# A Perceiver layer on one core: constant products in TensorE's fold, another order at its end, and row clearing moved into tile 0

## The reference

```python
# cross attention, 16 heads of 128
q_hk = (ln(x) @ Wq.T).reshape(b, s, H, K)
q_r = (q_hk @ w_kc_q) @ W_qr                   # 192, then 64 wide
kv_rope = kv_c * cos + rotate_half(kv_c) * sin # 257 rows of 64 for each batch
attn = softmax(q_r @ (kv_rope @ W_kr).T)
x = x + ((attn @ kv_rope) @ w_kc_kv.T).reshape(b, s, H * K) @ Wo.T
# self attention, weights are codes * scales (blocks of 32 rows)
x = x + softmax(q @ k.T / sqrt(128)) @ v @ wo + bo
# 64 experts, top 8, capacity 128: rows are scattered to their experts,
# put through gate, up and down, weighted and summed
x = x + moe(ln(x))
```

## Time and profile before

| | |
|---|---|
| median of 3 runs | 736.1 us (734.83 to 737.74) |
| profiled execution | 734.79 us |
| its span, first to last instruction | 733.0 us |
| PE busy | 631.6 us, 86% |
| DVE, ACT, POOL busy | 61%, 39%, 38% |
| mean granted clock of PE | 0.925 |
| chain that ended last | PE 52%, DVE 17%, issue 11%, ACT 8% |

### The profile page before, as it was taken

The page is one execution under the profiler, slowest core; times in us unless marked ns, Lnnn a source line. Parts: engine busy times, 40 slices in busy tenths (PEclk is TensorE's granted clock), DMA queues, the critical chain, the costliest instruction groups (busy, mean ns, idle before and its releaser), DMA issues.

```text
span 733.0 us, 16840 instructions
## 1 busy us (share of the span) xinstructions
PE 631.6 (86%) x6395; PEld 540.9 (74%) x6395; DVE 446.3 (61%) x1257; ACT 285.6 (39%) x788; POOL 275.1 (38%) x296
## 2 busy tenths in 40 slices
PE   5998687989989999999999999998886899999900
PEld 3887556977887896896897896896765688778800
DVE  1143696555677577677677677576573245555548
ACT  1112485336337337337347337346030043333300
POOL 3852599211212612612612612403103435555520
PEclk9556798999999999999999999999999999999965
DMA  7697551990400600500500200100002769998467
GB/s 192 191 250 185 164 190 35 293 325 4 138 2 2 199 2 9 193 2 10 192 3 10 77 3 10 56 3 31 32 4 86 203 196 334 330 318 277 131 254 296
DMA packets 90383, 95.85 MB, mean 131 GB/s; under 512 B 26047, under 2 KB 82104, under 8 KB 89280
## 3 DMA queue, kind: packets, MB, share of 16 engines
q1 hardware_dynamic: 83552, 78.40, 35.8%
q0 software_dynamic: 6144, 15.96, 6.0%
q10 hardware_dynamic: 608, 0.42, 0.2%
HBM read 60.19 MB, written 36.18 MB: 131 GB/s over the span
## 4 chain that ended last, share of the span: by engine, by line
PE 52%; DVE 17%; issue 11%; ACT 8%; DMA 4%; SPq 4%; POOL 2%; another core or an unknown queue 1%; POOLq 0%; DVEq 0%; ACTq 0%
PE bank L1258 6%; PE bank L1259 6%; PE bank L1260 6%; PE bank L1324 4%; PE bank L1292 3%; PE bank L1373 3%; PE bank L1278 3%; PE bank L1543 3%; PE bank L1313 3%; DMA Wh<-expert_rows 2%; POOL pair_rows L650 2%; ACT diag L735 2%; PE bank L1511 2%; ACT qspace L676 2%; DVE space L1212 2%
## 5 line engine op out<-in xcount | busy, mean ns | idle before, releaser
L697 ACT ACTIVATE pr<-bank,nmax 128x257 f32<-128x257 f32 x128 | 61.4, 480 | 95.5 <-DVE nmax L921 92.5
L574 POOL DMA_INDIRECT expert_rows<-h,slot x64 | 63.0, 984 | 69.4 <-DVE slot L1018 53.7
L1258 PE MATMUL bank<-space,Wh 128*128 128x128 f16 x512 | 88.1, 219 | 0.3
L1260 PE MATMUL bank<-space,Wl 128*128 128x128 f16 x512 | 88.1, 219 | 0.0
L1259 PE MATMUL bank<-space,Wh 128*128 128x128 f16 x512 | 88.1, 219 | 0.0
L557 POOL TENSOR_TENSOR Cr<-C,Ct 128x192 f32<-128x192 f32 x64 | 39.3, 636 | 122.4 <-PE bank L1324 113.3
L650 POOL DMA_INDIRECT pair_rows<-Wh,etok x64 | 62.4, 974 | 56.5 <-issue 36.2
L921 DVE TENSOR_REDUCE nmax<-bank 128x1 f32<-128x257 f32 x128 | 53.4, 421 | 43.0 <-PE bank L1306 30.1
L705 ACT COPY pT<-bank 128x256 f32<-128x256 f32 x128 | 47.6, 372 | 64.1 <-PE bank L1313 61.5
L1324 PE MATMUL bank<-Cr,pT 128*128 128x64 f32 x512 | 72.2, 264 | 0.1
L1324 PEld LDWEIGHTS bank<-Cr,pT 128*128 128x128 f32 x512 | 68.2, 194 | 0.2 <-ACT pT L705 0.2
(11 more groups left out here) (208 smaller groups left out, 1548.2 us busy)
## 6 DMA issues: line engine op xcount, KB each, us to landing
expert_rows<-h SPq DMA_DIRECT2D x8, 1120.0 KB, 13.3
Wh<-expert_rows SPq DMA_DIRECT2D x64, 140.0 KB
pair_rows<-zrow SPq DMA_DIRECT2D x8, 1024.0 KB
Wl<-L_ffn_gate_up_proj_dram SPq DMA_DIRECT2D x36, 192.0 KB
ring<-L_ffn_gate_up_proj_dram SPq DMA_DIRECT2D x28, 192.0 KB
space<-pair_rows SPq DMA_DIRECT2D x5, 1024.0 KB, 9.2
Wl<-L_ffn_down_proj_dram SPq DMA_DIRECT2D x36, 96.0 KB
C<-ctx_dram SPq DMA_DIRECT2D x24, 128.0 KB
```

What stands on the lines that cost most here:

```text
L574: e.indirect_dma_start(XE[:, :], bass.IndirectOffsetOnAxis(ap=slot[:, k:k + 1], axis=0), h3[:, :], None, bounds_check=E * CAP - 1, oob_is_ ...
L697: e.activation(pr[:, s, :], bank[r % 2][:, 0:NL], ACT.Exp, bias=nmax[:, s:s + 1], accum_out=rsum[:, s:s + 1]).then_inc(expd, 1)
L1258: e.matmul(dst, ah, bh, start=first and n == 0, stop=False)
L1260: ins = e.matmul(dst, al, bh, start=False, stop=last and n == len(terms) - 1)
```

## The change

It has six parts. PE: `keep_busy(n, to)` issues n products of two constant tiles (128 x 128, bfloat16) into `bank[1]`, which nobody reads; 4 between every two heads of the Q and M stages in all four groups (24 for each group), and 14, 14, 20 and 12 in rows 17 to 20 of tile 0. PE: `qb` moves from ahead of tile 0 to its row 2, behind the scores of rows 0 and 1. Parts: group 2 has part 0 alone, the last group parts 1 to 4, of which part 4's multiply and high half move into row 1 of tile 0 (DVE and ACT), ahead of `qb`'s low half on DVE; the multiplies of parts 1 and 2 now surround `kt0`'s low half. POOL: `rope_products(1)` moves from tile 0 to between the low halves of parts 0 and 1. SP: `load_context(1)` moves ahead of part 1's load, and the eight `blank` ahead of the wait for 16 parts and of the experts, each with a wait on `expd`. DVE: the split of `bv` moves into the last group.

```diff
+KEEP_AT = {17: 14, 18: 14, 19: 20, 20: 12}
-FOLD_PARTS = (0, 0, 2, 3)
+FOLD_PARTS = (0, 0, 1, 4)
# SP
             load_fold_first(3)
+            e.wait_ge(roped, 2 * BT)
+            load_context(1)
             load_part(1)
...
-            e.wait_ge(roped, 2 * BT)
-            load_context(1)
-
             e.wait_ge(f_m, GROUPS)
...
             load_codes(PARTS - 1, late[10], late_in[10])
 
-            e.wait_ge(w_done, PARTS)
-
...
+            e.wait_ge(iotas, 2)
+            for n in range(E // 8):
+                e.wait_ge(expd, 6 + 2 * n)
+                blank(n)
+
+            e.wait_ge(w_done, PARTS)
             for n in range(NB):
                 load_expert(n, n)
             for i in range(2, T):
 
                 e.wait_ge(roped, i * (2 * BT))
                 load_context(i)
-                if i == 2:
-                    e.wait_ge(iotas, 2)
-                    for n in range(E // 8):
-                        blank(n)
# POOL
-            for u in range(PART0[GROUPS]):
+            part_low(0)
+            rope_products(1)
+            for u in range(1, PART0[GROUPS]):
                 part_low(u)
...
-                if not last:
+                if not last and i != 0:
                     rope_products(i + 1)
# ACT
+                        if isinstance(i, int) and i == 0 and r == 1:
+                            x_use(XNEXT[-1], 0)
+                            part_high(LATE - 1)
...
-                for u in range(PART0[g], PART0[g + 1]):
+                for u in range(PART0[g], min(PART0[g + 1], LATE - 1)):
                     part_high(u)
-
-            x_use(XNEXT[-1], 0)
# DVE
+                        if isinstance(i, int) and i == 0 and r == 1:
+                            part_mul(LATE - 1)
+                            x_low(XNEXT[-1], 0)
...
                 if g == GROUPS - 1:
-                    for name in XNEXT[1:-1]:
-                        x_low(name, 0)
-                if len(left) > 2:
                     part_mul(left.pop(0))
+                    x_low("kt0", 0)
+                    part_mul(left.pop(0))
+                    x_low("qa", 0)
# PE
+            def keep_busy(n, to):
+
+                for _ in range(n):
+                    e.matmul(to[:, 0:P], ones16[:, :], before[:, :], start=True, stop=True)
...
+                        if isinstance(i, int) and i == 0 and r == 2:
+
+                            e.wait_ge(f_md, GROUPS)
+                            e.wait_ge(f_na, GROUPS)
+                            x_use("qb", 0)
...
+                        if isinstance(i, int) and i == 0 and r in KEEP_AT:
+                            keep_busy(KEEP_AT[r], bank[1])
...
# Q stage, and the same behind each head of the M stage
+                    if h < GH - 1:
+                        keep_busy(4, bank[1])
```

More of the change, by code:

```diff
@@ L1146, in _ @@
                     part_mul(left.pop(0))
+                if g == GROUPS - 1:
+                    e.wait_ge(rwT_ready, 3)
+                    e.tensor_copy(bvh[:, :], bvT[:, :]).then_inc(bv_split, 1)
+                    e.wait_ge(bv_split, 1)
+                    e.tensor_tensor(bvl[:, :], bvT[:, :], bvh[:, :], ALU.subtract).then_inc(bv_split, 1)
                 e.wait_ge(f_m, g + 1)
@@ L1152, in _ @@
                     next_h1(0)
-                for u in left:
-                    part_mul(u)
-            x_low(XNEXT[-1], 0)
+                if g < GROUPS - 1:
+                    for u in left:
+                        part_mul(u)
             e.sem_inc(h3_free, FREE)
             e.wait_ge(iotas, 2)
[L1160 to L1163, removed]
             tile(0, None, None)
@@ L1514, in _ @@
                     transposes(g + 1)
-            e.wait_ge(f_md, GROUPS)
-            e.wait_ge(f_na, GROUPS)
-            x_use("qb", 0)
             tile(0, None, None)
```

## The result

| | before | after |
|---|---|---|
| median | 735.47 us (734.19 to 737.74) | 751.9 us (749.25 to 756.88) |
| ratio of after to before | | 1.0202, 95% interval 1.0158 to 1.0246 |
| profiled execution | 734.79 us | 749.25 us |
| its span | 733.0 us | 747.5 us |
| mean granted clock | 0.925 | 0.930 |

The change makes the kernel 2% slower; the forecast was 745, range 735.5 to 752. The profiled executions differ by 14.46 us, and all but 0.6 of that is there at tile 1's out product.

The account below looks back on a forecast made before the run. The prediction took TensorE (PE), busy 86% of 733.0 us, as the bound, with POOL setting tile 0's length. Its terms, 0 + 2 + 0 - 2 + 12 + 2 - 5 = +9 us on 734.8, gave 743.8, written as 745; range 735.5 to 752.

Parts of the forecast that it names:

- (e): Head of tile 1: context load held behind clearings 6 and 7 delays POOL and PE; +12 us, ends 10 and 14.
- (f): Tile 1: PE idles some 11 us, and the clock is low behind that; +2 us, ends 0 and 3.
- (g): Tile 1: with no clearing at 155 us, the 3.14 us gap goes with its low clock; -5 us, other end 0.
- (d): End of tile 0: 14 products cost 0.8 us, out product goes 6.24 to 3.46 if clock holds; -2.0 us, else +4.
- (b): Fold's end: row 2's scores wait for part 4's load, its multiply and qb's low half; +2 us, ends -1 and +5.
- (c): Tile 0: moving tile 1's rope products off POOL there gains 0.3 us at most; taken as 0, else +1.
- (a): Fold groups 0 to 2: cost of 72 columns of constant products and clock gain cancel; 0 us, ends -3.5 and +7.7.
- What was said of the loads: Fold: the last group's weights aren't there before 50.0 us, so groups 0 and 1 can give only about 1 us.
- Rival 2: Fold: the clock stays at 1.2 GHz despite the products; (a) becomes +7.7, in all 751.5 us; chance 0.13.
- the rule beside it: Fold: the skill wants TensorE continuously busy for full clock; the trace showed it busy without a gap at 0.50.
- What the prediction said of transposes: Fold: a run of transposes was followed by a clock rise to 0.83, though the skill says they don't count as busy.

Follow-up runs that it names:

- six_early: The kernel after with SP's last two clearings (6 and 7) moved behind the experts and context 2; 736.58 us, ratio 0.9992 to the kernel before.
- clear_alone: The kernel before with only the eight clearings moved ahead of the wait for 16 parts and the experts; 745.24 us, ratio 1.0122.
- early_alone: The kernel before with only six of eight clearings moved ahead, numbers 6 and 7 behind context 2; 724.84 us, ratio 0.9950.
- weights_first: six_early with the loads of the last two fold groups' weights ahead of part 0's load on SP; 730.11 us, ratio 0.9917.
- no_fold_products: six_early without the 96 constant products of the fold, those of tile 0 kept; 727.04 us, ratio 0.9856.
- moved_products: no_fold_products with the 96 constant products put back in one piece ahead of row 2's scores of tile 0; 726.71 us, ratio 0.9987.
- qb_first: six_early with qb's low half ahead of part 4's multiply, and part 4's multiply and high half moved to row 2 of tile 0; 734.71 us, ratio 0.9913.
- clear_late: The kernel after with all eight clearings put back behind context 2; 738.83 us, ratio 1.0008 to the kernel before.
- no_products: The kernel after without any constant products, in the fold and in tile 0; 750.13 us, ratio 1.0144 to the kernel before.
- all_fold_kept: six_early with the edits of qb_first and weights_first, fold products kept, the 60 of tile 0 left out; 718.00 us, ratio 0.9872.
- all_three: six_early with the edits of qb_first and weights_first, and without the fold's constant products; 717.79 us, ratio 0.9860.
- no_tile_products: six_early without the 60 constant products at tile 0's end, those of the fold kept; 733.14 us, ratio 0.9969.

## Why the prediction was right, and where it wasn't

The sign and the mechanism that decides were right; the time, 751.9 instead of 745, lies 0.1 us inside the range. That it still lies inside is luck: four terms came out dearer than forecast and one cheaper. By the steps, for the two profiled executions (forecast, measured):

**(e) The late context: +12, measured 12.0.** PE waits 11.98 us. SP held by clearings 6 and 7, 16 expert issues ahead of context 2, POOL in order: each link is in the rows. six_early mends it by that link alone and gets 15 us back; clear_alone makes it by that link alone. That the number fits to the tenth is partly luck: for this wait by itself the forecast was 11.3, and its 12 took in some of the work that queues behind, which stands under (f) here.

**(f) The clock behind it: +2, measured 3.7.** C without wait or gap is 49.6 in five kernels; 65.24 - 49.6 - 11.98 = 3.7, clock and queued work of DVE together. This term was mis-sized, and the 3.7 lies above its end of 3; how it divides isn't shown. In clear_alone the same remainder is 2.6.

**(g) The gap: -5, measured -4.2,** which is 53.82 - 49.6. Its cause was taken rightly for the kernel before: early_alone removes the DMA traffic and the gap shrinks to 0.47 (one trace each). But the statement was incomplete. With 156 products more ahead of tile 1, in either of the two placements tried, there is another gap, 12 products before the end of the narrow group, which needs no DMA traffic. In the kernel after it is 0.27 us, as in this row of PE's timeline:

```profile
176.60 0.32 PE L1374 MATMUL bank<-space 128*32 128x32 f32 x12 [0.27 <-issue]
```

PE had idled 12 us shortly before. Without that wait the gap is 2.1 to 2.7 us, in five kernels, and C is 52.6 to 54.6 there.

**(d) Tile 0's end: -2.0, measured -0.8** (B, 10.55 to 9.79). The failed step is "if the clock holds": it had fallen in the 2.14 us wait ahead of the products (0.58 in 124 to 128 us), so the first 14 cost 1.49 us in the chain instead of 0.8. The condition itself was right. In three kernels (weights_first, no_fold_products, moved_products) the clock held at 1.00 through the same wait of 2.14 us, and B is 8.24, or -2.3; in the five others with the products it is 9.8 to 9.9, in the six without them 10.1 to 11.2. All fourteen kernels have this wait (2.13 or 2.14 us), so the wait alone doesn't decide whether the clock falls.

**(b) The fold's end: +2, measured +1.7** (A, 12.08 to 13.79), by the chain that was forecast, in which only the landing of part 4's load took longer (5.1 us behind the end of its issues, not 4.5); qb_first shows that this load was its link. **(c): 0, measured 0**: from row 2's scores to the start of B it is 33.60 us before and 33.61 after.

**(a) The fold's products: 0, measured +1.5** in these two executions (N's copy at 75.95 and 77.41; 0.7 of it stands under (b)). What was said of the loads held: PE took them up at 50.2, and between 48.9 and 51.5 us in all nine kernels with this order of loads in which it waited for them. But two traces don't size this term, since the fold's clock differs from run to run: clear_alone and early_alone have the fold of the kernel before unchanged, and N's copy stands at 79.34 and 78.92 there, 3 us and more behind the 75.95 of that kernel. By the ratios the 96 products cost 1.4% in six_early, 10 us (to within 4), of which 4.9 is tile 1's gap. The 5 left lie inside the ends -3.5 to +7.7, and rather above 0, the value taken; they don't settle it. In moved_products the products cost as much without standing in the fold.

Sum: 1.5 + 1.7 - 0.8 + 12.0 + 3.7 - 4.2 = 13.9, and 0.6 behind tile 1 make the 14.5 us. This accounts for two traces; of its terms, (e) and (g) are shown by experiments, and the 1.5 at (a) is within the spread of the fold. The forecast had 9 and missed 1.5 at (a), 1.2 at (d), 1.7 at (f) and 0.8 at (g), less 0.3 at (b). The median lies 2.7 us above the profiled execution, where the forecast had added 1.3.

**Rival 2 and the rule beside it.** The clock of the fold is not settled by its products. clear_late has them, and by stretches PE is busy without a pause at 0.50:

```profile
52.00:56.00 4.00, 4.00 (x26) 4.00 (x26) 1.34 (x3) 0.00 (x0) 0.00 (x0) 0.50 0.76 193
56.00:60.00 4.00, 4.00 (x20) 2.75 (x20) 0.42 (x1) 0.58 (x1) 0.00 (x0) 0.50 1.09 172
```

no_products has none and shows 1.00 in 36 to 40 us. early_alone, whose fold is that of the kernel before, has none in it either, and reaches 0.89; by stretches:

```profile
32.00:36.00 4.00, 4.00 (x31) 3.09 (x30) 2.02 (x4) 0.96 (x2) 3.85 (x3) 0.89 0.85 223
```

It then waits 3.60 us for `W_kr`, and clear_alone 2.90. So neither the full clock in the kernel after's fold nor its wait of 4.33 us is shown to come from the products. The reason given for 0 at (a), that gains and payments cancel, is not shown either. A high stretch often ended in the wait for `W_kr`, but in all_fold_kept, which has no such wait, 40 to 44 us is at 0.50 too. The Trainium skill, "TensorE: Matmul & The Clock Gate", section "Why this matters for your kernels", wants TensorE busy continuously for the full clock. clear_late's rows are busy for 8 us at half clock with the constant products among them; in weights_first PE is busy from 24 to 56 us at 1.00, as the rule has it. So being busy doesn't forecast the clock here. What the prediction said of transposes stays open: no run varies them.

## What to carry to other kernels

When a step is moved ahead in an in-order DMA queue, work out what its own wait holds back: here two of eight clearings, waiting for rows of the next tile, cost 2%, and placed behind one small load they cost next to nothing. A faster stage is worth what the next stage's loads allow, so move these first. And products added only to hold the clock also shift all code behind them: check the engine's gaps without a releaser, far downstream, before and after.

## What the runs showed of the hardware

**A gap that belongs to a place in the program.** In six_early, clear_late, qb_first, weights_first and moved_products PE stops for 2.50, 2.69, 2.11, 2.44 and 2.47 us behind the 116th of 128 products of 32 columns. In all five PE's program has 156 more products ahead than in the kernel before; with 60 or 96 of them left out tile 1 has no gap over 0.6 us. The kernel before has its gap 26 products later, 12 of the narrow group and 14 behind it. Counting two instructions for a product (its weight load and itself), the added 156 are 312, less the 52 between the two places are 260. The Trainium skill, "Runtime: NRT & Kernel Launch", section "Instruction fetch mechanics", says that an engine's code is refilled in blocks of 256 instructions over a DMA queue of its own, mostly hidden. By this count, which leaves out waits, the two places fit such blocks to within 4 instructions; no run shows the refill itself. If the gaps are refills, "mostly hidden" doesn't hold here: at the 116th product 2.1 to 2.5 us with idle DMA engines and 2.69 with full ones, at the other place 3.14 with full and 0.47 with idle ones. But crossing a block is not enough. By the same count a block would end near the 82nd of the 128 products in no_fold_products and all_three, and near the 46th in no_tile_products and all_fold_kept, and there no two starts are over 0.02 us apart. What must be added stays open. One candidate is the rate: the group uses up its instructions fastest, 116 products in 1.19 us. With the wait of 12 us in row 4 of the tile the gap at the 116th product is 0.27 (the kernel after).

**Chips.** The kernel before has medians of 735.75, 739.12 and 728.55 us in series 1, 2 and 3. From tile 1's out product to the end of the span it is 539 to 542 us in the four traces of series 3 and 545 to 552 in all others, so times of different series are compared above by their ratios alone.
